# Attention and ternary FFN on eight cores: the weight transposes of the first pass moved one chunk later

## The reference, cut to what matters

```
def attn(x, Q, K, VO):                      # x: 4 x 4096 x 1024, Q and K: 64 x 1024, VO: 1024 x 1024
    xq = x @ Q.T; xk = x @ K.T
    return softmax(xq @ xk.T / 32) @ (x @ VO)

def ffn(x, weight):                         # weight: 1024 x 1024
    w_scale = mean(|weight|) + 1e-8
    w_quant = clip(round(weight / w_scale), -1, 1)
    a_scale = max(|x|, axis=-1) + 1e-8
    a_quant = round(clip(x / a_scale * 127, -128, 127))
    return (a_quant @ w_quant.T) * (w_scale * a_scale / 127)

x = x + attn(layernorm(x), Q, K, VO)
x = x + ffn(layernorm(x), weight)
```

## Time and profile before

| | us |
|---|---|
| time before, median of 3 runs | 725.63 (724.71 to 725.81) |
| the profiled execution, its own time | 723.71 |
| its span on the slowest core, core 7 | 722.2 |
| spans of the eight cores | 709.8 to 722.2 |
| PE busy | 565.2 (78% of the span) |
| DVE busy | 509.2 (71%) |
| ACT busy | 260.5 (36%) |

### The profile page before, as it was taken

One profiled execution on the slowest core, in us unless ns is written; L12 is line 12 of the kernel. 1 busy time (PEld: TensorE's weight loads), 2 busy tenths in 40 slices (PEclk: granted clock), 3 DMA queues, 4 the chain that ended last, 5 costly groups with the idle time before them and its releaser, 6 DMA issues.

```text
span 722.2 us, 9675 instructions; the slowest of 8 cores (709.8 to 722.2 us)
## 1 busy us (share of the span) xinstructions
PE 565.2 (78%) x3284; PEld 274.3 (38%) x3284; DVE 509.2 (71%) x824; ACT 260.5 (36%) x491; POOL 9.3 (1%) x22
## 2 busy tenths in 40 slices
PE   1269998677777889898798898798798897898803
PEld 0035554343333434434343343343344343343401
DVE  4215454556665028889889898889898898889882
ACT  1445676242322514414414324325225235134100
POOL 0000000000000000000000000000000000000000
PEclk9989999898988997999998999999989999989955
DMA  4723464332333000100101101001001001000000
GB/s 120 221 97 110 174 188 142 117 117 88 105 104 142 1 24 7 59 27 32 59 3 57 50 9 59 29 30 60 29 30 59 29 30 59 29 30 30 0 29 30
DMA packets 12881, 47.29 MB, mean 65 GB/s; under 512 B 1440, under 2 KB 1440, under 8 KB 12832
## 3 DMA queue, kind: packets, MB, share of 16 engines
q1 hardware_dynamic: 10528, 38.28, 16.4%
q0 software_dynamic: 2304, 8.39, 2.9%
HBM read 38.27 MB, written 8.39 MB: 65 GB/s over the span
## 4 chain that ended last, share of the span: by engine, by line
DVE 45%; PE 30%; issue 11%; DMA 9%; ACT 2%; DVEq 1%; SPq 1%; POOL 0%; ACTq 0%; POOLq 0%
DVE sbuf_s L583 14%; PE ps_a L467 10%; PE ps_a L302 9%; DVE cbuf L579 8%; DMA wstg<-ww 5%; DMA wstg<-vo 3%; DVE hb L503 3%; DVE st L541 3%; PE ps_t L286 2%; DVE sbuf_s L574 2%; DVE aq L279 2%; DVE outb L631 2%; DVE st L510 2%; DVE hn L537 2%; PE ps_kq L614 2%
## 5 line engine op out<-in xcount | busy, mean ns | idle before, releaser
L467 PE MATMUL ps_a<-V,PT 128*128 128x512 bf16 x1024 | 242.8, 395 | 1.8 <-ACT PT L458 1.8
L467 PEld LDWEIGHTS ps_a<-V,PT 128*128 128x128 bf16 x1024 | 102.0, 102 | 120.8 <-issue 18.0
L583 DVE TENSOR_TENSOR sbuf_s<-sbuf_s,cbuf 128x1024 f32<-128x1024 f32 x112 | 137.2, 1225 | 11.6
L302 PE MATMUL ps_a<-VOc,xnT 128*128 128x512 bf16 x512 | 126.9, 404 | 21.3 <-ACT VOc L168 19.8
L579 DVE TENSOR_SCALAR cbuf<-sbuf_s 128x1024 f32<-128x1024 f32 x112 | 77.8, 694 | 12.6 <-DVE sbuf_s L574 0.5
L458 ACT COPY PT<-ps_t 128x1024 bf16<-128x1024 bf16 x64 | 64.4, 1012 | 59.0 <-PE ps_t L453 59.0
L603 ACT COPY aqT<-ps_t 128x512 bf16<-128x512 bf16 x32 | 17.2, 590 | 184.4 <-PE ps_t L597 184.4
L302 PEld LDWEIGHTS ps_a<-VOc,xnT 128*128 128x128 bf16 x512 | 51.3, 103 | 84.2 <-issue 37.3
L614 PE MATMUL ps_kq<-wqT,aqT 128*128 128x512 bf16 x256 | 66.9, 421 | 9.4 <-ACT aqT L603 9.4
L279 DVE TENSOR_SCALAR aq<-xstg,st 128x1024 bf16<-128x1024 f32 x32 | 25.9, 811 | 66.6 <-ACT st L270 38.5
L312 ACT CAST V<-ps_a 128x512 bf16<-128x512 f32 x64 | 34.4, 590 | 71.6 <-PE ps_a L302 71.6
(11 more groups left out here) (81 smaller groups left out, 459.2 us busy)
## 6 DMA issues: line engine op xcount, KB each, us to landing
xstg<-xb SPq DMA_DIRECT2D x32, 512.0 KB, 4.3
wstg<-ww SPq DMA_DIRECT2D x16, 512.0 KB, 5.2
xres<-xb SPq DMA_DIRECT2D x16, 512.0 KB, 3.3
y<-outb POOLq DMA_DIRECT2D x16, 512.0 KB, 2.9
wstg<-vo SPq DMA_DIRECT2D x8, 512.0 KB, 4.8
xres<-qw SPq DMA_DIRECT2D x1, 256.0 KB, 4.1
xres<-kw SPq DMA_DIRECT2D x1, 256.0 KB, 5.2
```

Source lines behind the costliest of these rows:

```text
L302: last = e.matmul(ps_a[eh], xnT[par][:, 128 * j:128 * j + 128], VOc[:, 1024 * j + 512 * eh:1024 * j + 512 * eh + 512], start=(j == 0), sto ...
L467: last = e.matmul(ps_a[eh], PT[:, 128 * kb:128 * kb + 128], V[:, 1024 * kb + 512 * eh:1024 * kb + 512 * eh + 512], start=(kb == 0), stop=( ...
L583: S.emit("vector", lambda e: e.tensor_tensor(out=sbuf_s[:], in0=sbuf_s[:], in1=cbuf[:], op=OP.subtract), reads=["s_a", "s_b", "cbuf"], wri ...
```

## The change

In each odd turn the transposes of the chunk before are emitted ahead of the vector work of the present chunk. So chunk co is quantised in turn 17 + 2co as it was, but transposed and copied in turn 19 + 2co, just before chunk co+1 is quantised; the last chunk is transposed behind the matmuls of tile 31. The number of instructions and of loads stays the same.

```
--- before.py
+++ after.py
@@ -363,9 +363,13 @@
                     wabs_chunk(i - 8)
                 if i == 8 + DC:
                     wscale_finish()
+                if i >= 19 and i % 2 == 1 and (i - 19) // 2 < DC - 1:
+                    wquant_tp((i - 19) // 2)
                 if i >= 17 and i % 2 == 1 and (i - 17) // 2 < DC:
-                    wquant_chunk((i - 17) // 2)
+                    wquant_v((i - 17) // 2)
         p1_mm(nt - 1)
+        if interleave:
+            wquant_tp(DC - 1)
         if not interleave:
             for j in range(DC):
                 wabs_chunk(j)
```

## The result

The changed kernel takes 736.6 us (median of 8 runs, 735.4 to 737.9), the kernel before 725.2 (8 runs beside it, 723.2 to 726.1). The ratio is 1.0162, its 95% interval 1.0147 to 1.0178: 1.6% slower, 11.4 us by the medians. The profiled execution took 735.47 us, its longest span is 733.5.

The account below looks back on a forecast made before the run. Bound: a loop through weight-chunk load, DVE and PE, PE having slack. First turn -1.96, six pairs of 17.16 and an end of 17.0 put the score matmul 12.6 later; with 0.2, +12.8 on 725.63 gives 738.4 us (733 to 742.5).

Parts of the forecast that it names:

- The removed wait wasn't booked as gain: First pass: PE's waits for `aqT` all go, but PE had slack in the loop, so no gain is counted.
- The wait moves to L234: Odd turns: DVE stands at the copy for PE's matmuls of tile i-1, 5 to 7 us a time, quantising queued behind.
- 15.16 us a pair at the higher clock: Weight-chunk part: a pair (two tiles, one chunk) sums to 15.16 us from rows of before, without clock loss.
- The excess of 2.0 us in every pair: Even to odd tile's transposes take 2.0 us above 4.55, from PE's lowered clock; a pair takes 17.16 us.
- The rival that it stays at 1.39: Second rival: time above 4.55 us between even and odd transposes keeps its old mean, 1.39; +8.5, 734.1 us; chance 15%.
- no excess: First rival: no clock loss, pairs of 15.16 us, 1.2 us faster, 724.4 us; chance 4%.
- the third rival: Clock loss per pair near the longest seen, 2.86 us; +18.8, 744.4 us; chance 8%.
- The first turn: Chunk 0's turn: normalisation no longer behind transposes and copy; 1.96 us gained, even transposes at 137.39 on core 0.
- The end, 0.6 and 0.2 us: End of first pass: chunk 7's transposes cost 0.6 us; its copy delays the score matmul's reduction by 0.2.
- Entry to the score matmul on the slowest core: First pass, core 0: from even transposes at 137.39 to the score matmul at 257.4, 12.6 later than core 7 before.
- The cores lie closer together: Across cores: they should lie closer together than before, as the load no longer sets their pace; no size given.
- The fourth rival: Copy doesn't hold DVE, the load ends last; some 1.55 us less a pair, 715.5 us; chance 3%.

Follow-up runs that it names:

- the order experiment: Changed kernel with only DVE's order altered: new chunk quantised before the old one is copied, quantised chunk in two buffers; 719.0 us, ratio 0.9907 to the kernel before.
- the filling: Changed kernel plus 20 useless PE matmuls behind each chunk's transposes: all but the last chunk, 730.6 us; repeated for chunks 0 to 5 only, 726.3 us.
- The second experiment: Changed kernel with the old chunk's transposes on PE ahead of tile i-1's matmuls, in the even tiles' PSUM tile; 718.1 us, ratio 0.9883 to the kernel before.
- the early load: Each weight chunk's load issued one pair earlier: in the kernel before 705.2 us, again 703.9; in the changed kernel 731.6 us.

## Why the prediction was right

The time was forecast at 738.4 us and came out at 736.6, +12.8 against +11.4. The mechanism is the one forecast; the closeness of the number is in part luck, as two of the points below say.

- *The removed wait wasn't booked as gain.* PE's waits for `aqT` did go, all of them; the time rose. Right, and shown by the order experiment: PE's list unchanged, the time lower by more than the loss.
- *The wait moves to L234, with the quantising queued behind it.* Right: 36.4 us in six pairs, as forecast 5 to 7 us a time, and taking it away from either side (719.0, 718.1) brings the pairs back to where the load sets them.
- *15.16 us a pair at the higher clock.* Forecast from rows of before; measured 15.16 with the filling. In the second pair it was 15.52 on all cores: 0.36 more, between L210 and the quantising behind it (a wait of 0.5 us of DVE for itself, once), which no term had.
- *The excess of 2.0 us in every pair.* Measured: 54 of 56 pairs have one, mean 1.80; the two without are first pairs, which follow turn 17's stall and not the new one. Over the 48 behind the new stall the mean is 1.87. The rival that it stays at 1.39 is out, and so are no excess and the longest one; the forecast by the nine long waits was nearer than the mean over all 56. Two readings in this part of the prediction are off. The longest excess of before is not 2.86 but 2.95 us (158.58 less 151.08 less 4.55, core 6), which would put the third rival at 745.1. And not all 23 waits were shorter than the new stall: one was 5.55 us. Neither changes the forecast.
- *The first turn.* The gain of 1.96 us is there to the hundredth. The load of chunk 0 lands at other times in each execution, so it has to be read from L219 on: from there to the even tile's transposes it was 4.06 us on core 7 (137.97 less 133.91), and it is 2.10 (136.64 less 134.54), 2.09 or 2.10 on all eight cores. How late the load lands was not forecast. I took core 0, the last to enter before; core 7 ended last now and had entered at 136.64 instead of the 137.39 forecast. That is 0.8 of the 1.5 us by which its span grew less (11.3) than the 12.8 forecast.
- *The end, 0.6 and 0.2 us.* 250.65 to 255.60 is 4.95 as forecast, then 0.54 to the score matmul. Its reduction on DVE starts 0.78 us behind it instead of 0.50, so the delay is there; but the span behind the score matmul is 477.4 us as before, and the 0.2 us was not to be added.
- *Entry to the score matmul on the slowest core:* 120.0 forecast, 119.5 measured (256.14 less 136.64). Two errors stand against each other in it: core 7's seven excesses add up to 13.2 us instead of 14.0, and the 0.36 us of the second pair was not in the sum. The second pass took 477.4 us in both.
- *The cores lie closer together.* Right, but by less than the profiled executions show (5.7 us wide against 12.4): over nine executions of the changed kernel the mean width is 7.2 us, over 32 of the kernel before, timed beside the experiments, 9.9. That the load no longer sets their pace fits this; it isn't shown to be the reason.
- *The fourth rival,* that the load ends last and the copy holds nobody, needed the copy ready early. The second experiment made it so on purpose and got 718, near the 715.5 that the rival had for that case.

On the Trainium skill (TensorE: Matmul & The Clock Gate, section on HAM oscillation), by which a burst behind a long wait of PE starts at the lower clock: the traces agree with it in all 48 pairs behind the new stall (PE waits 5.06 us in them, 5.42 in eight). Where the filling left waits of 1.2 us or less, none of the 48 pairs of either run has an excess, which doesn't go against the section, since its case is long waits for loads.

What stays open: why a pair of before with a short wait for `aqT` had the excess in 18 of 33 cases and not in the others. No run was made for it. The two profiles of the early load in the kernel before show one side: where PE didn't wait for `aqT` at all and stood only the 1.67 us ahead of the even tile, 3 of 95 pairs have an excess; where it also waited 0.2 to 1.8 us for `aqT`, 7 of 17 have one. So the 1.67 us alone rarely brings it.

## What to carry to other kernels

Moving work of one engine later to spare it a wait puts the consumer's work later too: look at what stands first in the consumer's queue, and what is queued behind it. Ask first which wait closes the loop; here it was a load, and issuing it earlier gave 3%, while the change took away a wait that had slack. The same transposes one chunk later did save time (719.0 and 718.1 us) once the quantising no longer stood behind PE's matmuls. A stall gathered in one place costs more than its length when the clock falls behind it: 5.07 us of stall cost another 1.9 each time.

## What the runs showed of the hardware

The pairs of the changed kernel run together to one length on all cores, from both sides. On core 3 they are 18.05, 17.93, 17.15, 17.10, 17.09, 17.07 us, on core 1 16.43, 17.11, 16.73, 16.89, 16.98, 17.03; with the early load, core 6 goes from 18.44 to 17.11. With the filling, at the granted clock of 1.00, there is nothing to run together: the third to fifth pairs are 15.15 to 15.17 us on every core of both runs. So in these two kernels the excess isn't scattered around its mean, it settles at 1.9 us.
